# A two-layer kernel whose first attention projects the values of two pairs of heads by seven block products, with the weights split in place

## The reference

```python
qkv = silu(hidden @ qkv_w.T)              # 32 heads of 128, each with q, k, v
scores = einsum(q, k) * diag_decay        # blocks of 32 tokens, a running kv state
out = scores @ v + (q * q_decay) @ kv
normed = norm_w * out * rsqrt(mean(out * out) + eps)
return (sigmoid(hidden @ gate_w.T) * normed) @ out_w.T
```

## Time and profile before

| what | value |
|---|---|
| median of 3 runs | 2613.15 us (2606.18 to 2614.91) |
| the profiled execution | 2614.36 us |
| its span, first to last instruction | 2612.5 us |
| granted TensorE clock, mean | 0.99 |
| PE busy | 2539.0 us |
| GpSimd (POOL) busy | 1351.8 us |
| VectorE (DVE) busy | 1120.3 us |
| ScalarE (ACT) busy | 1095.1 us |

### The profile page before, as it was taken

One profiled execution on the slowest core, in us unless ns is written; L12 is line 12 of the kernel. 1 busy time (PEld: TensorE's weight loads), 2 busy tenths in 40 slices (PEclk: granted clock), 3 DMA queues, 4 the chain that ended last, 5 costly groups with the idle time before them and its releaser, 6 DMA issues.

```text
span 2612.5 us, 40008 instructions
## 1 busy us (share of the span) xinstructions
PE 2539.0 (97%) x13674; PEld 2183.6 (84%) x13674; DVE 1120.3 (43%) x1881; ACT 1095.1 (42%) x2070; POOL 1351.8 (52%) x1355
## 2 busy tenths in 40 slices
PE   7999999999999999999999999999999999969999
PEld 6888888888888888778888888888888888847777
DVE  6333333333333334763333333333333488864553
ACT  5443444344434443443434443444344357733332
POOL 5655555555555552766555555555555378731210
PEclk9999999999999999999999999999999999979999
DMA  4211111111111111311111111111111079931110
GB/s 157 96 51 46 46 48 60 46 46 46 52 54 46 46 47 57 115 56 53 47 46 46 49 60 46 46 46 52 54 46 47 15 246 304 301 108 46 33 33 33
DMA packets 73730, 187.70 MB, mean 72 GB/s; under 512 B 12163, under 2 KB 15891, under 8 KB 73671
## 3 DMA queue, kind: packets, MB, share of 16 engines
q1 hardware_dynamic: 65126, 170.13, 19.3%
q0 software_dynamic: 8544, 16.82, 2.2%
HBM read 168.00 MB, written 26.79 MB: 75 GB/s over the span
## 4 chain that ended last, share of the span: by engine, by line
PE 84%; DVE 7%; ACT 4%; issue 2%; DMA 2%; POOL 1%; ACTq 0%; SPq 0%; DVEq 0%; POOLq 0%
PE bank L96 23%; PE bank L97 23%; PE bank L98 23%; PE bank L985 4%; PE bank L971 4%; PE bank L987 2%; PE bank L972 2%; DVE el L2095 2%; ACT exth L2055 1%; ACT eh L2066 0%; DVE ehf L2107 0%; DMA l_stage<-y_slots,slot_of 0%; DMA y_slots<-ey 0%; POOL l_stage L2614 0%; ACT eh L2060 0%
## 5 line engine op out<-in xcount | busy, mean ns | idle before, releaser
L96 PE MATMUL bank<-xh,wh 128*128 128x512 f32 x1400 | 559.0, 399 | 0.0
L98 PE MATMUL bank<-xh,wl 128*128 128x512 f32 x1400 | 546.2, 390 | 0.0
L1686 POOL TENSOR_TENSOR wl<-raw,wh 128x512 fp32r<-128x512 f32 x196 | 252.4, 1302 | 157.6 <-ACT wh L1239 155.0
L97 PE MATMUL bank<-xl_sums,wh 128*128 128x512 f32 x800 | 315.5, 394 | 0.0
L98 PEld LDWEIGHTS bank<-xh,wl 128*128 128x128 f32 x1400 | 263.1, 188 | 57.0
L96 PEld LDWEIGHTS bank<-xh,wh 128*128 128x128 f32 x1400 | 263.5, 188 | 52.9 <-ACT bank L1194 0.3
L1494 DVE TENSOR_TENSOR acc<-bank,acc 128x512 f32<-128x512 f32 x240 | 165.8, 691 | 317.3 <-PE bank L98 317.3
L96 PE MATMUL bank<-wh,xh 128*128 128x256 f32 x1024 | 293.7, 287 | 3.4 <-DVE xl L504 3.4
L1451 DVE TENSOR_TENSOR ms<-bank,dcur 128x384 f32<-128x384 f32 x256 | 142.4, 557 | 354.5 <-PE bank L972 345.1
L98 PE MATMUL bank<-wh,xl 128*128 128x256 f32 x1024 | 291.2, 284 | 0.0
L97 PE MATMUL bank<-wl,xh 128*128 128x256 f32 x1024 | 291.1, 284 | 0.0
(11 more groups left out here) (347 smaller groups left out, 5338.2 us busy)
## 6 DMA issues: line engine op xcount, KB each, us to landing
raw<-in_w_pairs_dram SPq DMA_DIRECT2D x128, 512.0 KB, 3.9
raw<-in_o_pairs_dram SPq DMA_DIRECT2D x32, 512.0 KB, 3.1
eraw<-in_ex_dram SPq DMA_DIRECT2D x31, 513.0 KB
y_slots<-ey SPq DMA_DIRECT2D x31, 512.0 KB
dcur<-in_decay_dram SPq DMA_DIRECT2D x32, 384.0 KB, 3.0
eraw<-in_ex_dram SPq DMA_DIRECT2D x31, 256.0 KB
out_dram<-acc SPq DMA_DIRECT2D x16, 256.0 KB, 2.1
l_raw<-in_l_w_dram SPq DMA_DIRECT2D x28, 116.0 KB
```

What stands on the lines that cost most here:

```text
L96: pe.matmul(out, wh, mh, start=start and i == 0, stop=False, skip_group_check=True)
L97: pe.matmul(out, wh, ml, start=False, stop=False, skip_group_check=True)
L98: ins = pe.matmul(out, wl, mh, start=False, stop=stop and i == n - 1, skip_group_check=True)
L1686: pool.tensor_tensor(wl[:, cols], src, wh[:, cols].bitcast(F32), ALU.subtract).then_inc(w_lo, 1)
```

## The change

- The values of two pairs (2m and 2m + 1) are projected together, in even rounds from 2 on, by two sections j = 3 and 4 of seven products each; section j = 3 + i covers tiles 2i and 2i + 1 of both token blocks. Each product is 2 tiles x 2 chunks x 3 passes of 256 columns. Pairs 0 and 1 keep the plain form. The odd pair's values are kept in vt_odd, in places of xh and xl that the products do not read.
- wh and wl have four equal places of 7 blocks each. The raw weights arrive in wl's own place (w_in is the same memory), all sums are formed there, and GpSimd's subtraction overwrites them. raw0, raw1 and wsum go; the output weights get a buffer o_in of their own. q, k, g, v, v0 and v1 move round the four places.
- SyncE's weight DMAs wait for the last product of the place (pe_p) instead of for GpSimd.
- All engines loop over two rounds at a time, an even and an odd one (m = 1 to 6 looped, m = 7 written out).
- ScalarE's casts and GpSimd's blocks stand at other points of the round: in odd rounds and round 1 q's first two casts come ahead of section 2's "ab" and the other two and k's in section 2; in even rounds v0's come in section 1, v1's in section 2, q's in section 3, k's in section 4.

```diff
+    w_in = nc.alloc_sbuf_tensor_at("w_in", [P, 4 * WSEC], F32, offset=wl_at)
...
+    def add_up(pool, place, done, n):
+
+        blk = [w_in[:, place * WSEC + i * WBLK:place * WSEC + (i + 1) * WBLK] for i in range(7)]
+        pool.tensor_tensor(blk[S3], blk[A11], blk[S1], ALU.subtract).then_inc(done, 1)
+        pool.wait_ge(done, n + 1)
+        pool.tensor_tensor(blk[S1], blk[S1], blk[A22], ALU.add).then_inc(done, 1)
...
+    PLACE = {"front0": {"q": 0, "k": 1, "g": 2, "v": 3}, "front1": {"q": 0, "k": 1, "g": 2, "v": 3},
+             "first": {"q": 0, "k": 1}, "second": {"g": 2, "v": 3, "q": 0, "k": 1},
+             "even": {"g": 2, "v0": 3, "v1": 0, "q": 1, "k": 2}, "odd": {"g": 3, "q": 0, "k": 1}}
...
             def all_rounds(eng, run):
 
-                run(0)
-                with eng.Fori(1, UNITS - 1) as n:
-                    run(n)
-                run(UNITS - 1)
-                run(UNITS)
+                run(FIRST)
+                run(SECOND)
+                with eng.Fori(1, UNITS // 2 - 1) as m:
+                    run(Round("even", m))
+                    run(Round("odd", m))
+                run(Round("even", UNITS // 2 - 1))
+                run(Round("odd", UNITS // 2 - 1))
+                run(END)
```

SyncE (cut):

```diff
+                    if r.even:
+                        wait(sp, pe_p, r.products)
+                        bring_values(sp, r, 0)
+                    if not r.first:
+                        wait(sp, w_lo, r.o_ready())
+                    sp.dma_start(o_in[:], o_pairs[n]).then_inc(dma_o, 16)
...
+                    wait(sp, pe_p, product_n(r, 0, 4))
+                    if r.even:
+                        bring_values(sp, r, 1)
...
+                    else:
+                        bring(sp, r, "q", pair_section(n + 1, 0))
```

PE, a value product and the end of a round:

```diff
+                    if j >= 3:
+                        for i in range(2):
+                            t = 2 * (j - 3) + i
+                            tok = slice(t * P, (t + 1) * P)
+                            parts = []
+                            for c in range(2):
+                                m = slice(r.place(f"v{c}") * WSEC + a * WBLK, r.place(f"v{c}") * WSEC + (a + 1) * WBLK)
+                                parts.append((xh[:, b, c, tok], xl(b)[:, c, tok], wh[:, m], wl[:, m]))
+                            ins = three_passes(pe, pj[BANK[k]][:, i * WBLK:(i + 1) * WBLK], parts, k in (1, 5) and i == 0,
+                                               True)
...
+                    if r.even:
+                        section(r, 3, *ORDER)
+                        section(r, 4, 1, 5)
+                    scores(r, 0)
+                    scores(r, 1)
...
+                    if r.even:
+                        section(r, 4, *ORDER[2:])
```

ScalarE around section 2 and at the end of an even round, and GpSimd:

```diff
+                    take(r, 1, "b")
+                    if r.second or r.odd:
+                        split(r, "q", 0, 1)
+                    take(r, 2, "ab")
...
+                        split(r, "q", 2)
+                    take(r, 2, "t5")
...
+                        split(r, "q", 3)
+                        split(r, "k", 0, 1)
...
+                    if r.even:
+                        for j, what in ((3, "q"), (4, "k")):
+                            take(r, j, "ab")
+                            split(r, what, 0)
+                            take(r, j, "t5")
+                            split(r, what, 1, 2)
...
+                    add_squares(u, 3)
+                    if r.even:
+                        low(r, "v1")
+                    else:
+                        low(r, "q")
+                        low(r, "k")
...
+                    low_o(r)
...
+                    if r.even:
+                        low(r, "q")
+                        low(r, "k")
```

## The result

The changed kernel takes **2638.94 us** (median of 4 runs, 2632.62 to 2639.82) where the kernel before took 2610.08 beside it (4 runs, 2606.18 to 2614.91): 1.0104 times as long, 95% interval 1.0078 to 1.013. It is slower. The forecast was 2626 us, within 2580 to 2645, with 0.52 for slower.

What follows compares the result with a forecast made beforehand. PE, busy 97% of the span, was taken to bound the kernel. 2614.4 - 40.3 - 1.2 + 32.0 + 8.8 + 13.6 = 2627.3 us, by the median 2626 us; range 2580 to 2645.

Steps and rivals of the forecast that it cites:

- The saving: PE's value products: 168 matmuls instead of 192 per two pairs, 14 x 24 x 0.120 = 40.3 us less.
- Rival (5): Value products in groups of 12 run 0.017 us a matmul slower, so the saving is gone: 2666 us, chance 0.05.
- Odd and second rounds: Section 2: copy ab waits behind q's casts and GpSimd's additions, product 6 starts 2.0 us late, 16 times: 32.0 us.
- Section 3: Even rounds: t5 stands behind q's first cast, so VectorE's sum makes product 7 0.63 us late, 14 times: 8.8 us.
- The clock: PE's clock halves after 8 of the 16 section 2 gaps, losing 1.7 us each: 13.6 us, ends 0 and 27.
- rivals (1) and (2): The loop's clock never falls: 2612 us, chance 0.15; or it falls after each gap: 2640 us, chance 0.12.
- The same round of the second half ... keeps that: Second round, second half: PE's wait for VectorE's routing, 3.17 us, stays as it was.
- Nothing that follows in the section is waiting as long: Section 2, odd and second rounds: k's casts hold ScalarE until about 619.4, but PE needs them only a section later.
- The costs at nothing: The g block, v0, v1, weight loads and SyncE's queue: ready before PE needs them, so priced at no time.
- Rival (3): Blocked ScalarE is absorbed: 16 blocks cost 0.5 us each, section 3's nothing; 2580 us, chance 0.26.
- Rival (4): Two-round loop body: late instructions at 12 jumps, up to 3.9 us each, 47 us; taken at 2650 us, chance 0.05.
- -1.2 for the beginning: Start of the kernel: gaps at 50.13 and before 104.39 go, together about 1.2 us less.

Runs made afterwards that it cites:

- the kernel with only section 3 edited: The changed kernel, with ScalarE making copy t5 before the first cast of the weights in sections 3 and 4 of even rounds: 2622.25 us, ratio 1.0039.
- the kernel with both edits: The changed kernel with GpSimd's additions of q's block ahead of the last squares, and copy t5 ahead of the casts in sections 3 and 4: 2566.75 us.

## Why the prediction was right

The sign, the place and the mechanism came out. The size came out only as far as the range: 2638.94 us is 13 us above the forecast, and the slowdown itself was forecast as 13 us and measured as 25.5 between the profiled executions, 28.9 between the medians. Of those 13 us, 8.2 are one term, the stall of the odd rounds.

- **The saving, 40.3 us:** 39.9 measured by putting the matmuls back. Rival (5), that groups of 12 run slower, is refuted with it.
- **Odd and second rounds, 16 x 2.0 = 32.0 us:** right in the mechanism (the casts ahead of the copy, the additions behind the squares: each edit removes it), wrong in the size. The stall is 2.44 us, and 2.60 or 2.80 in six rounds of the second half, 40.2 us in all. The mis-sized term is "four additions take 3.19 us": they take 3.64, since the first has 1.20 us in place of 0.74 beside VectorE's yl. In the earlier trace rows the first of them had 0.74 too. In the second half the same chain is later by another 0.17 us or more: there GpSimd's last sum of squares starts 0.27 us behind the end of ScalarE's square (1431.51 and 1431.24), in the first half 0.08 (368.28 and 368.20). What holds GpSimd there stays open.
- **Section 3, 14 x 0.63 = 8.8 us:** 0.64 us by the starts, 0.73 a pair when it was removed, 10 us.
- **The clock, 8 of 16 falls at 1.7 us = 13.6:** 9 falls at 1.6, 14.4 us. The number was luck in part: the kernel with only section 3 edited has the same gaps and had 5. The caution that one row is thin for a rule was right: the gap of 1.87 us of the earlier trace rows stands in all 11 kernels profiled (1.85 to 1.87), and the clock fell behind it in six and not in five. In the six, the kernel before among them, PE had stood for another 1.20 to 1.72 us some 7 us earlier; in the five for 0.32 us or less. So the row showed two gaps close together, not one. As to the loop, rivals (1) and (2), never and always, are both refuted for this kernel.
- **"The same round of the second half ... keeps that":** a step that failed. I priced the routing's 3.17 us gap as unchanged. GpSimd's additions and subtractions of g came beside VectorE's small operations, and the gap grew by 2.1 us.
- **"Nothing that follows in the section is waiting as long":** true only under cover of the stall. With the copy moved ahead and the additions left late, k's casts cost PE about 0.6 us a pair. In the kernel with the additions first this is gone too.
- **The costs at nothing** (g, v0, v1, the loads, the queue of SyncE) hold in the even and odd rounds: the kernel with both edits has no gap over 0.3 us there.
- **Rival (3)**, the block absorbed, fell: the price was paid 16 times. Its point of decision was right, though. With GpSimd's additions done earlier nothing is lost, and the time is then 2577 us, where the rival had 2580.
- **Rival (4)**, the longer loop: pairs of 120.57 us are 123.50 - 2.93, so the jumps cost nothing to be seen (the last pair of a half, written out without a jump, takes 120.49). The stall that the Trainium skill warns of (Runtime: NRT & Kernel Launch, Instruction fetch mechanics) doesn't show here.

The sum, against the profiled execution of before, whose span is 2612.5: -40.3 + 40.2 + 9.0 + 14.4 + 2.1 - 1.2 for the beginning = +24.2 us; the spans differ by 25.5. The -1.2 is borne out: the first cast of oh in the second round comes at 125.05 us where it came at 123.86, 1.19 later with a stall of 2.44 ahead of it.

## What to carry to other kernels

Price a saved stretch of the bounding engine only together with the queues that must now be on time: here 40 us were saved and 64 given back, clock included, at 30 places where a cast stood ahead of a short copy in a queue of fixed order. When such a cast waits, look at the waiting engine's supplier before its own order: putting the additions into GpSimd's idle 8.9 us gained more than moving the copy (61.6 and 47.8 us by the medians). Two engines' work that is moved side by side needs a row in which they were side by side, for its duration.

## What the hardware showed unexpectedly

VectorE and GpSimd slow each other, and the small operations most in proportion. A 128x32 operation of VectorE went from 0.18 us to 1.16 to 1.22 beside GpSimd's subtractions, which take 4.53 / 4 = 1.13 us each: about the length of one of them. GpSimd's addition of 256 columns went from 0.74 to 1.20 us beside yl, and it is 0.74 again where the edit of the additions takes it away from yl. In both halves' attention of the changed kernel 59 of the 60 such additions that overlap yl take 1.17 to 1.29 us (the other overlaps it for 0.08 us); 163 beside VectorE operations that read or write PSUM take 0.72 to 0.76, as long as those beside none. The Trainium skill (SBUF — State Buffer, SBUF: two separate sides) has the two engines share one pair of ports as an exclusive lock, held for a whole instruction, in certain forms of VectorE's operations; these durations, and the 0.18 us once GpSimd waited, agree with it.

TensorE's clock fell from 2.4 to 1.2 GHz after some of a row of equal gaps and not after others: after 9 and 5 of 16 at 2.27 to 2.63 us, after none of ten at 1.75, after 14 of 16 at 2.78 to 3.17, with the longest among the exceptions. A stall of this size has to be priced with its share of falls, about 0.3 to 0.9 of 1.6 us here, and the kernels without the large gaps had none in their loop. What decides between two equal gaps stays open.
